# experts_0 to attention_1 by halves of the rows, with the next stage's first weights split inside the loop over the experts

## What is computed

```python
x = x + _L0_ffn_ref(_layernorm(x, axis=-1), ...)   # 8 experts, 2 per token, and one shared expert
x = x + _L1_attn_ref(_layernorm(x, axis=-1), ...)  # the call normalises once more:

mu = jnp.mean(h, axis=-1, keepdims=True)
var = jnp.mean(jnp.square(h - mu), axis=-1, keepdims=True)
x = (h - mu) * jax.lax.rsqrt(var + EPS) * ln_g + ln_b
q = (x @ wq.T + bq).reshape(b, s, N_HEADS, D_K)    # 16 heads of 128; k and v likewise
q = rope(q); k = rope(k)
attn = jax.nn.softmax(jnp.where(causal, -jnp.inf, q k^T * scale), axis=-1)
return (attn v) @ wo.T + bo + residual
```

## Time and profile before

| | us |
|---|---|
| median of 3 runs | 1021.71 |
| lowest and highest | 1018.13, 1022.21 |
| profiled execution | 1020.11 |
| its span | 1018.3 |
| busy: PE, PEld | 968.0 (95%), 800.8 (79%) |
| busy: DVE, ACT, POOL | 719.4 (71%), 598.4 (59%), 422.7 (42%) |

### The profile page before, as it was taken

The page is one execution under the profiler, slowest core; times in us unless marked ns, Lnnn a source line. Parts: engine busy times, 40 slices in busy tenths (PEclk is TensorE's granted clock), DMA queues, the critical chain, the costliest instruction groups (busy, mean ns, idle before and its releaser), DMA issues. The chain is left out here.

```text
span 1018.3 us, 20957 instructions
## 1 busy us (share of the span) xinstructions
PE 968.0 (95%) x7053; PEld 800.8 (79%) x7053; DVE 719.4 (71%) x2156; ACT 598.4 (59%) x1515; POOL 422.7 (42%) x412
## 2 busy tenths in 40 slices
PE   8899999999998998999998899999999998899988
PEld 6677778777876654877777788989888987788877
DVE  6777777777764568663368677778776786569994
ACT  2177777777775675232133877777777864335433
POOL 5767666767664301146532634445344431110000
PEclk9999999999999999999999999999999999999999
DMA  5360222122000200652230401101010100001111
GB/s 173 74 209 22 64 53 49 27 64 43 2 1 9 105 1 2 213 149 84 78 114 7 151 18 31 36 15 41 26 31 26 26 12 1 1 1 47 47 38 51
DMA packets 27640, 54.53 MB, mean 54 GB/s; under 512 B 4534, under 2 KB 14902, under 8 KB 25846
## 3 DMA queue, kind: packets, MB, share of 16 engines
q1 hardware_dynamic: 25350, 47.44, 16.3%
q0 software_dynamic: 2208, 6.03, 2.0%
HBM read 38.90 MB, written 6.16 MB: 44 GB/s over the span
## 5 line engine op out<-in xcount | busy, mean ns | idle before, releaser
L525 ACT ACTIVATE sb_a_P<-sb_a_nS,sb_a_nm 128x257 f32<-128x257 f32 x256 | 127.6, 507 | 86.3 <-DVE sb_a_nm L636 86.1
L435 POOL TENSOR_TENSOR sb_a_P<-sb_a_P,sb_a_rec 128x512 f32<-128x512 f32 x128 | 129.2, 1040 | 87.6 <-DVE sb_a_rec L647 87.5
L636 DVE CUSTOM_DVE_ANT_0 sb_a_nS<-a_pS,sb_a_mask,sb_a_nsink 128x256 f32<-128x256 f32 x256 | 109.3, 479 | 39.0 <-PE a_pS L784 39.0
L2229 ACT ACTIVATE sb_a_t<-a_pp,sb_a_w 64x512 f32<-64x512 f32 x128 | 87.6, 684 | 13.8 <-PE a_pp L144 6.0
L2301 DVE SCALAR_TENSOR_TENSOR sb_a_t<-a_pp,sb_a_w,sb_a_cs 128x512 f32<-128x512 f32 x64 | 47.8, 747 | 56.8 <-ACT sb_a_t L2229 56.8
L2153 POOL TENSOR_TENSOR sb_a_qT<-sb_a_t 128x512 f32<-128x512 f32 x32 | 41.2, 1288 | 108.9 <-DVE sb_a_t L2304 108.9
L144 PE MATMUL a_pp<-sb_x_high,sb_a_w_low 128*128 128x512 f32 x184 | 78.3, 425 | 7.7 <-DVE sb_a_P L591 4.8
L144 PE MATMUL a_pp<-sb_x_high,sb_a_w_high 128*128 128x512 f32 x184 | 72.8, 396 | 0.0
L144 PE MATMUL a_pp<-sb_x_low,sb_a_w_high 128*128 128x512 f32 x184 | 72.6, 395 | 0.0
L534 ACT COPY sb_xn<-a_pT 128x512 f32<-128x512 f32 x128 | 68.0, 583 | 1.9 <-PE a_pT L798 1.9
L798 PE MATMUL a_pT<-sb_ident,sb_a_P 128*128 128x128 f32 x512 | 68.2, 276 | 0.3 <-ACT sb_xn L534 0.3
(11 more groups left out here) (463 smaller groups left out, 2901.5 us busy)
## 6 DMA issues: line engine op xcount, KB each, us to landing
sb_a_kr<-sb_a_kall SPq DMA_DIRECT2D x28, 256.0 KB, 4.3
sb_f_w<-f_w SPq DMA_DIRECT2D x12, 384.0 KB, 2.9
sb_a_w<-a_w SPq DMA_DIRECT2D x16, 257.0 KB, 2.7
sb_m_egu<-m_egu SPq DMA_DIRECT2D x2, 1408.0 KB, 11.1
sb_a_w<-a_w SPq DMA_DIRECT2D x8, 259.0 KB, 2.7
sb_a_wo<-a_wo SPq DMA_DIRECT2D x8, 256.0 KB, 2.7
sb_a_wv<-a_wv SPq DMA_DIRECT2D x8, 256.0 KB, 2.7
sb_a_wo<-a_wo SPq DMA_DIRECT2D x16, 128.0 KB, 2.0
```

What stands on the lines that cost most here:

```text
L435: nc.gpsimd.tensor_tensor(part, part, rec[b % 2][:, h, :].rearrange("p (q o) -> p q o", o=1) .to_broadcast([P, 2, S]), ALU.mult).then_inc( ...
L525: out = nc.scalar.activation(Pm[b % 2][:, h, qt, 0:S + 1], nS[:, h, qt, 0:S + 1], ACT.Exp, bias=nm[b % 2][:, h, qt:qt + 1], scale=-1.0, ac ...
L636: out = nc.vector.tensor_tensor_reduce(nS[:, h, qt, 0:S], pS[h][:, qt * S:(qt + 1) * S], wmask[:, qt, :], -1.0, nsink[par][:, h:h + 1], AL ...
L2229: out = nc.scalar.activation(t2[n][a, :, :].rearrange("p b s -> p (b s)"), pp[n][b, :], ACT.Identity, bias=bias[b])
```

## The change

Six edits.

1. The four weight splits move into the loop over the experts, one after each of the pairs 3, 5, 7 and 9. Their low parts are made on VectorE instead of GpSimd.
2. In tile LAST of experts_0, half 1's first four additions come between the two halves of `times_up`, the other four after `h_low`.
3. The scaling of half 0 moves from attention_1 into experts_0, the statistics of half 1 from experts_0 into attention_1.
4. The opening of attention_1 goes by halves: turn half 0, q and k chunk of half 0, turn half 1, the two value chunks (tiles 0 to 3), then q and k chunk of half 1. Each chunk of head 0 has a bank of its own, each rotated one its own buffers t1 and t2. The queues of ScalarE, VectorE and GpSimd follow this order.
5. The additions of bo leave the opening for GpSimd's queue in heads 13 and 14 (`base`).
6. M0_BUSY 26 to 22, A1_BUSY 16 to 10.

```diff
-A1_BUSY = 16
+A1_BUSY = 10
-M0_BUSY = 26
+M0_BUSY = 22
...
+    def scale(self, nc, dve, k, half):
+        dve.wait_ge(self.rstd_ready, 4 * half + 2)
+        for t in range(half * HALF, (half + 1) * HALF):
+            nc.vector.tensor_scalar(k.xn[:, t, :], k.x[:, t, :], k.mv[:, t, 0:1], self.root2[:, 1, t:t + 1],
+                                    ALU.subtract, ALU.mult).then_inc(self.xn_ready, 1)
...
+        SPLIT_AT = (3, 5, 7, 9)
...
-            low(first.w_high, 1, w_of(0), first.ws[0], first.w_split)
-            low(first.wv_high, 2, k.tile["a1_wv0"][:, :], first.wvs, first.wv_split, 2)
-            low(first.w_high, 2, w_of(1), first.ws[1], first.w_split)
-            low(first.wo_high, 1, k.tile["a1_wo0"][:, 0:D], first.wos[0], first.wo_split)
...
                         if j + 1 < PAIRS:
                             turned_rows(j + 1)
+                        if j in SPLIT_AT:
+                            first_weight_high(SPLIT_AT.index(j))
...
                         if j > 0:
                             products_of_pair(j - 1)
+                        if j - 1 in SPLIT_AT:
+                            first_weight_low(SPLIT_AT.index(j - 1))
...
-                if n > 0:
+                if n == LAST:
+                    times_up(n, (0,))
+                    add_products(1, ((0, 0),))
+                    times_up(n, (1,))
+                    down_low(n)
+                    h_low(n)
+                    add_products(1, ((1, 2),))
+                elif n > 0:
...
-                dve.wait_ge(added, (half + 1) * HALF)
-                row_stats(nc, dve, k, k.x, first.ln, 0, half)
-            dve.wait_ge(first.ln, 4 * HALF)
+                if half == 0:
+                    dve.wait_ge(added, HALF)
+                    row_stats(nc, dve, k, k.x, first.ln, 0, half)
+            first.scale(nc, dve, k, 0)
+            dve.wait_ge(added, NT)
+            dve.wait_ge(first.xn_ready, HALF)
...
+        first_banks = {0: pp[0], 2: pp[1], 4: pY, 5: pO[1], 1: pS[0], 3: pT}
+        PROJECTED, ROTATED = [0, 2, 4, 5, 1, 3], [0, 2, 1, 3]
...
+            def base(H, b):
+                pool.wait_ge(added, H * A1_U + b + 1)
+                for t in (2 * b, 2 * b + 1):
+                    nc.gpsimd.tensor_tensor(k.x[:, t, :], k.x[:, t, :], bo[:, :], ALU.add).then_inc(based, 1)
...
                 project(H + 1, 1 - par, (0, 1))
                 if par == 1:
                     low(wv_high, H + 3, wv[:, :], wvs, wv_split, 2)
+                if isinstance(H, int) and H == A1_H - 2:
+                    base(H - 1, 2)
+                    base(H - 1, 3)
                 project(H + 1, 1 - par, (2, 3))
...
                 wo_low(H + 1, 1 - par)
+                if isinstance(H, int) and H == A1_H - 3:
+                    base(H, 0)
+                    base(H, 1)
...
-            project(0, 0)
-            for t in range(NT):
-                pool.wait_ge(grown_x, t + 1)
-                nc.gpsimd.tensor_tensor(k.x[:, t, :], k.x[:, t, :], bo[:, :], ALU.add).then_inc(based, 1)
+            project(0, 0, ROTATED)
...
+            turned_row(0)
+            turned_row(2)
+            act.wait_ge(affine, 2)
+            high_row(0)
+            high_row(2)
+            swap(0, 0, 0)
+            swap(0, 0, 2)
+            turned_row(3)
+            act.wait_ge(affine_by_vector, 1)
+            high_row(1)
+            act.wait_ge(affine, 3)
+            high_row(3)
+            grow(range(0, 3))
+            swap(0, 0, 1)
+            swap(0, 0, 3)
+            grow(range(3, NT))
...
+            row_stats(nc, dve, k, k.x, first_head.ln, 0, 1)
+            low_row(0)
+            low_row(1)
+            shift_rows(0)
+            first_head.scale(nc, dve, k, 1)
...
+            rope(0, 0, 0)
+            dve.wait_ge(turned, 2)
+            nc.vector.tensor_scalar(part_of(k.xT, 1), turn_banks[1][:, :], cols_of[:, 0, 0:1], cols_of[:, 1, 0:1],
+                                    ALU.mult, ALU.add).then_inc(affine_by_vector, 1)
+            low_row(2)
+            low_row(3)
+            rope(0, 0, 2)
+            shift_rows(1)
+            rope(0, 0, 1)
+            rope(0, 0, 3)
...
+            first_chunk(0)
+            chunk_of(0, 0, 2)
+            turn_half(nc, pe, k, turn_banks, xn_ready, 0, turned, 1)
+            chunk_of(0, 0, 4)
+            chunk_of(0, 0, 5)
+            first_chunk(1)
+            chunk_of(0, 0, 3)
```

More of the change, by code:

```diff
@@ L1572, in h_high_of, with first_weight_high @@
                     high_of(nc, hs[n % 2][0][:, h * NC:(h + 1) * NC], hT[h][:, :]).then_inc(h_high, 1)
[L1574 to L1580, removed]
+            def first_weight_high(i):
+                if i == 0:
+                    k.wait(act, "a1")
+                    high_of(nc, first.ws[0][0][:, :], k.tile["a1_w0"][:, 0:2 * KD * P]).then_inc(first.w_high, 1)
+                elif i == 1:
+                    high_of(nc, first.wvs[0][:, :], k.tile["a1_wv0"][:, :]).then_inc(first.wv_high, 2)
+                elif i == 2:
+                    high_of(nc, first.ws[1][0][:, :], k.tile["a1_w1"][:, 0:2 * KD * P]).then_inc(first.w_high, 1)
+                else:
+                    high_of(nc, first.wos[0][0][:, :], k.tile["a1_wo0"][:, 0:D]).then_inc(first.wo_high, 1)
             def turned_rows(j):
@@ L1749, in shares, with first_weight_low @@
                 nc.vector.tensor_tensor(share[:, :, 2:3], eg[:, :, 0:1], share[:, :, 0:1], ALU.mult).then_inc(share_ready, 1)
+            def first_weight_low(i):
+                if i == 0:
+                    k.wait(dve, "a1")
+                    dve.wait_ge(first.w_high, 1)
+                    low_of(nc, first.ws[0][1][:, :], k.tile["a1_w0"][:, 0:2 * KD * P], first.ws[0][0][:, :]).then_inc(first.w_split, 1)
+                elif i == 1:
+                    dve.wait_ge(first.wv_high, 2)
+                    low_of(nc, first.wvs[1][:, :], k.tile["a1_wv0"][:, :], first.wvs[0][:, :]).then_inc(first.wv_split, 2)
+                elif i == 2:
+                    dve.wait_ge(first.w_high, 2)
+                    low_of(nc, first.ws[1][1][:, :], k.tile["a1_w1"][:, 0:2 * KD * P], first.ws[1][0][:, :]).then_inc(first.w_split, 1)
+                else:
+                    dve.wait_ge(first.wo_high, 1)
+                    low_of(nc, first.wos[0][1][:, :], k.tile["a1_wo0"][:, 0:D], first.wos[0][0][:, :]).then_inc(first.wo_split, 1)
             def up_of_pair(j):
@@ L2085, in wo_arrived, with rotated_in, opening, turn_of @@
                 eng.wait_ge(wo_in[par], 16 * (H // 2) + 16 * par)
+        def rotated_in(X, c):
+            if opening(X):
+                return first_banks[c], t1_first[c], t2_first[c]
+            return pp[c % 2], t1[c % 2], t2[c % 2]
+        def opening(X):
+            return isinstance(X, int) and X == 0
+        def turn_of(X, c):
+            return ROTATED.index(c) + 1 if opening(X) else X * 4 + c + 1
         CHUNKS = {1: {0: (0, 1), 1: (2, 3), 2: (4,), 3: (5,)},
@@ L2095, in filled @@
         def filled(X, c):
+            if opening(X):
+                return PROJECTED.index(c) + 1
             return X * 6 + (c + 1 if c < 6 else c - 1)
@@ L2266, in step @@
                         high_of(nc, OT[u % 2][0][:, :], pO[u % 2][:, 0:2 * P]).then_inc(OT_high, 1)
-            for c in range(4):
-                swap(0, 0, c)
-                grow(c)
+            turned_row(0)
[14 more added lines that the diff above has]
+            grow(range(3, NT))
             heads(act, step)
@@ L2320, in values @@
                 n = c - 4
+                bank = first_banks[c] if opening(X) else pp[c % 2]
                 if not (isinstance(X, int) and X < 2):
@@ L2339, in add_y @@
                 dve.wait_ge(rec_ready, H * A1_U + (u + 1))
-                if before(H, u, 1):
-                    dve.wait_ge(based, NT)
+                if before(H, u, A1_U):
+                    dve.wait_ge(grown_x, 2 * u + 2)
+                if isinstance(H, int) and H == A1_H - 2:
+                    dve.wait_ge(based, 2 * u + 2)
                 if not before(H, u, A1_U):
@@ L2411, in chunk_of @@
                         pe.wait_ge(v_ready, X * 2 + (c - 1))
-                else:
+                elif not opening(X):
                     pe.wait_ge(taken, X * 4 + (c - 1 if c < 6 else c - 3))
```

91 lines of the change are left out of this document (32 added, 59 removed).

## The result

The changed kernel takes 1015.23 us (median of 8 runs, lowest 1013.59); the kernel before, measured beside it, 1020.27 us (8 runs, 1018.13 to 1023.47). One of the eight runs of the changed kernel took 5411 us, for a reason that no record shows, and is left out of the ratio; the other seven have a median of 1015.21 and reach up to 1017.90. The ratio is 0.9952, with a 95% interval of 0.9934 to 0.9970: 4.9 us less, between 3.1 and 6.7. A later set on another chip gave 1015.59 against 1018.65, ratio 0.9964 (0.9945 to 0.9984). The forecast was 1016.1 us, a gain of 4.8.

What follows compares the result with a forecast made beforehand. TensorE was 95% busy, but the prediction took waits at the experts_0 to attention_1 seam as what the change touches. Terms -2.95 - 2.65 - 0.4 + 0.9 + 0.3 = -4.8 us gave 1016.1 us, range 1012.5 to 1019.8.

Steps and rivals of the forecast that it cites:

- Tail: End of experts_0: splits off GpSimd and reordered additions let VectorE finish at 544.7 instead of 547.66, 2.95 us less.
- Rival (e): Second group of expert rows lands after 532.2, tail keeps its length; costs up to 2.9 us, chance within (a)'s 0.22.
- Splits in the loop: Pair loop of experts_0: 0.6 us delay of the hidden-row copy hides in 1.65 us of slack; price 0, uncovered 2.4.
- Rival (c): Pair loop: GpSimd's DMA issues lock out VectorE's splits, net +12 us, 1033; chance 0.06.
- The split at 515.82: Pair loop, kernel before: a split not lengthened at 0.68 us beside a GpSimd issue of 1.17, cited against lock-out.
- Opening: Start of attention_1: working by halves, with fewer fillers, brings head 0's scores forward, 2.65 us less beyond the tail's gain.
- the product of 1.18: Opening, chunk 3's rotation: second VectorE product meets GpSimd's addition of chunk 1; forecast 0.45 us longer than 0.68.
- Rotation of head 0: Head 0: moving eight bias additions out of GpSimd's queue stops them lengthening a rotation product; gain 0.4 us.
- Half clock at the scores: Head 0's scores: TensorE's 4.7 us idle brings half clock, costing between 0 and 1.6 us; taken as 0.9.
- Heads 13 and 14: Moved bias additions in GpSimd's queue may delay rotations and last scores; between 0 and 1.7 us, taken as 0.3.
- Rival (a): Opening held by clock and port: transposes +0.9, scores +0.7, heads 13 and 14 +0.9; gain 2.3 us, 1018.6; chance 0.22.
- Rival (b): Larger gain: half clock falls on TensorE's idle time and nothing collides; -6.5 us, 1014.4; chance 0.13.

Runs made afterwards that it cites:

- e2: Kernel before with only the four weight splits moved into the pair loop, lows on VectorE; tail 19.16 us against 20.27 before.
- e3: Changed kernel with the four weight splits back on GpSimd behind the pair loop; tail 19.70 us against 17.03 in the changed kernel.
- e4: Changed kernel with two banks and two buffer pairs for head 0's four rotated chunks instead of four; opening 18.15 us against 18.16.
- e1: Changed kernel with 18 filler products on TensorE ahead of head 0's scores; first head 21.44 us against 22.90.
- e6: Changed kernel with each split one pair earlier, after pairs 2, 4, 6 and 8; last pair of the loop 18.10 us against 18.35.
- e7: Changed kernel with the eight bias additions back behind head 0's chunks on GpSimd; first head 23.35 us against 22.90, end 22.23 against 21.84.
- e9: Changed kernel with two already satisfied waits more on ScalarE directly ahead of the heads; heads 242.86 us against 243.42, first head 23.55 against 22.90.
- e11: Changed kernel with splits back on GpSimd, and two satisfied waits each on ScalarE and VectorE at the splits' loop places; last pair 17.72 us against 18.35.
- e10: Changed kernel with 18 fillers before the scores, splits one pair earlier, two satisfied ScalarE waits ahead of head 0's swaps; 1013.86 us, ratio to before 0.9940.
- e8: Changed kernel with 18 fillers before head 0's scores and splits one pair earlier, no added waits; first head 21.45 us against 22.90, heads 243.48.

## Why the prediction was right, and where it was not

- *Tail, forecast -2.95, measured -3.24.* The mechanism holds (e2, e3). The second silu ends 6.25 us after the first addition (forecast 6.30), and what lies behind it takes 10.1 instead of 10.3: only hand-overs that I had rounded up. Rival (e), late expert rows, is refuted: no addition waits for a DMA.
- *Splits in the loop, forecast 0, measured +0.76.* This term was mis-sized. The pairs in the middle do hide the splits (4.97 us, one 5.10), as the slack of 1.65 said. But I took that slack from the middle of the loop and carried it to its end, where the last pair holds one slot instead of two and TensorE's turn is 3.42 us. There the slack of the copy is nothing, and the last split's 0.34 goes straight into TensorE's idle time (0.83 for 0.49). Splits one pair earlier remove that wait, yet give back only 0.2 to 0.3 of the 0.76; where the remaining 0.4 to 0.5 arises stays open.
- *Rival (c), splits locked out by GpSimd*, is refuted: the three full splits take 0.68 each and the short one 0.42. It is the issue that pays: 1.16 instead of 0.97 when it begins inside a split. The split at 515.82, which I had taken for an undisturbed meeting, lay beside such an issue, of 1.17. The 0.2 on GpSimd that the forecast allowed for came at one of the four places.
- *Opening, forecast -2.65, measured -2.50.* Right in its steps: full clock at the transposes, scores 18.16 us after the stage's start against 18.0, the product of 1.18 by the port (0.50 for my 0.45). That the banks were a part of this was not in the sum, and e4 shows it is not.
- *Rotation of head 0, forecast -0.4, measured -0.43* between kernels at full clock.
- *Half clock at the scores, forecast +0.9, measured +1.46* (e1; 1.0 to 1.9 over the executions). Mis-sized: I put one stretch of half clock of 3.4 us there, partly over idle time, and in the changed kernel's profiles it lasts 6.8 us, 5.0 of them with TensorE at work in the first. The evidence was thin: the earlier trace rows had one stretch behind one idle of 2.78, and this idle was 4.7. Its length alone does not settle it either: e3, e4 and e6 stand idle 4.62 to 4.71 at the same place and have 3.4 us of half clock, the changed kernel, e7, e9 and e11 4.70 to 4.72 and have 6.8.
- *Heads 13 and 14, forecast +0.3, measured 0*: with e9's stream the heads and the end together take 264.70, before 264.74.
- *Not in the forecast: +0.55 in the loop over the heads*, by the place of ScalarE's instructions (e9, e10 against e8, e11 against e3). No row of the kernel before showed it, since there the gap is 0.12 in all turns.

The sum by these: -3.24 + 0.76 - 2.50 - 0.43 + 1.46 + 0.55 = -3.4. The second set of runs gives 3.7 by its ratio, the first 4.9; within the scatter of the runs both agree with 3.4. That the first set lies within 0.1 of the forecast's 4.8 is luck: the large terms, tail and opening, are right in mechanism and size, but the splits, the clock and the place of ScalarE's instructions cost 1.9 us more than forecast, of which the tail and heads 13 and 14 gave back 0.3 each. Rival (a) had named nearly the full cost of the clock; its other two parts did not come. Rival (b) is out, since the half clock fell on working time and the product of 1.18 did collide.

## What to carry to other kernels

Look for two-input VectorE work beside GpSimd work (additions of 1.67 us took 5.27 beside splits of 5.2): moving one of them removes it, but reorder what then becomes late, or most of the gain goes into the next wait (1.1 alone, 3.2 together). When a stretch is made shorter, ask what TensorE does meanwhile; a gap of 4.7 us cost 1.0 to 1.9, and eighteen fillers took it away and cost nothing (opening 18.22 against 18.16 to 18.22). Take the slack that is to hide a moved step from the very turn in which it will lie, the last turn above all.

## What the runs showed of the hardware that I had not expected

**The place of an instruction in ScalarE's stream changes when a loop's turn resumes.** Two satisfied waits ahead of a loop, or eight in an earlier stage, change starts of 0.41 and 0.20 us after the releasing instruction into 0.12 (e9, e10, e11; e4 with its two waits more has 0.12 too), 0.5 to 0.6 us in the stage's loop. The Trainium skill ("Runtime: NRT & Kernel Launch", section "Instruction fetch mechanics") says that instructions are fetched in blocks and that a taken branch whose target isn't in the window must wait for the fetch. The dependence on the place agrees with this; the fetch itself is in no row here, so it stays a reading and is not shown.

**The table load of ScalarE moves with waits.** In the changed kernel and in e10 it stands ahead of the wait for the maxima, at 560.40 and 560.22, and is free. In e9, with two waits directly ahead of the loop, it stood behind that wait, and the first exponential 1.4 us behind its maxima.

**An indirect DMA issue that begins inside a VectorE split takes 0.2 us longer.** The scatter's issue took 1.16 to 1.20 us instead of 0.97 to 1.00 wherever it began 0.36 us into a split of 0.68 with two SBUF inputs, in every kernel with the splits in the loop (once in the changed kernel, three times in e1 and e2). The split stayed at 0.68, and an issue that had begun before the split stayed at 0.96.
